# Causal attention: queries, keys and maxima brought to their rows by DMAs

## The chip, the cores and the metric

One core of a Trainium2 chip runs the whole program. The metric is the device time of one execution in microseconds (us), the median over runs of the same kernel. The engines are TensorE (PE in the profile; PEld is its weight load), VectorE (DVE), ScalarE (ACT), GpSimd (POOL) and SyncE (SP, which here only issues DMAs).

## The reference, cut to what matters

The program is a model of four layers; each adds two branches to x. Only the last layer's causal attention is touched:

```
q, k, v = heads(xn @ Wq.T), heads(xn @ Wk.T), heads(xn @ Wv.T)   # B = 2, S = 2048, 16 heads of 16
scores  = where(causal, q k^T * 16**-0.5, -inf)
out     = softmax(scores) v                                      # then the output projection, added to x
```

Beside it the layer's other branch ("phase") adds sqrt((xn cos)^2 + (xn sin)^2) to x.

## The kernel before, in words

Layer 3 (`layer3`, from line 2219) works through NJ = 8 groups j of four heads (four groups to each of the two sequences), and in each through NQ = 4 blocks n of 512 query positions. A pair (j, n) is called a unit here. Each unit is worked on twice.

`prep(j, n)` makes the unit's queries and keys and finds the row maxima of the scores. One product on PE (`pe_qk`, four PE instructions on f32 data) gives a 128x512 tile with 64 query rows and 64 key rows. ACT rounds it to fp32r (`hi`) and DVE takes the rest (`lo`), so that a product of 16-row heads can be made exactly enough from hi and lo parts. These rows then have to stand at other partitions: head hh of pair pr at partitions 64*hh onward of QS (queries) and KS (keys), as 16 rows each of hi, lo, hi for the queries and hi, hi, lo for the keys. `pe_place` does that with products by a selection matrix `Sel`: for each of queries (col 0) and keys (col 1), two pairs pr, and for each a product with hi and one with lo, so four products of 128x512 in a group; `act_place` evicts the two results of a group to QS or KS (and adds a one to the keys' spare rows). Then 8n+8 steps follow: in each, PE makes two 128 x up to 512 tiles of scores (two heads side by side, 64 rows of the array each) and DVE reduces each to its row maximum (L2592, and L2595 on the diagonal, with the causal mask `past`). Every maximum stands in a column of `pm`. At the end of a pair, `dve_maxima` writes the negated maxima into a wide bf16 tile `mz`, `pe_max` (L2358) turns them with four products by the identity, and `dve_max` (L2575) adds the resulting 128x512 tile from PSUM to the query rows, where row 48 of a head meets the ones of the keys. So the second pass gets score minus maximum from the product itself.

`main(j, n)` is the second pass: for each block kt of 128 keys up to the diagonal, four products K^T Q (64 rows of the array each, two side by side), four Exps on ACT (L2743), a causal mask on POOL for diagonal blocks, four products with the values (L2414), and at the unit's end the division by the sum and the output projection, added to x on DVE.

The order is written out by hand as generators. `weave_units` first runs `first()` (values, and prep of j = 0, all four n) beside the phase branch; then for each unit it weaves main(j, n) with prep(j+1, n) in fixed proportions; the last j has no prep beside it. `beside(n, step)` says what goes with which step of prep: at step 1 the next unit's qk product, at step 2 the maxima of the unit before (pair 1), at the half and one later the placing of the next unit's queries and keys, at half + 3 the maxima of pair 0. For n = 0 the unit's own placing stands in front of the steps, and for n = 3 no next unit is placed. All engines run their programs in order, and all products share a ring of seven PSUM banks (`psx`), each of which must be emptied before it is filled again. SP does nothing in this stage but store the output.

## Time and profile before

| | |
|---|---|
| median of 3 runs | 4099.81 us (4099.64 to 4100.76) |
| profiled execution | 4113.66 us, its span 4111.9 us |
| PE busy, of the span | 3689.5 us (90%) |
| DVE busy | 2578.5 us (63%) |
| ACT busy | 1742.1 us (42%) |
| POOL busy | 1087.5 us (26%) |
| granted PE clock, mean | 0.943 |
| attention, from the first placing to the end | 2962.8 us to 4111.9 us |

Busy time is the time in which an engine had an instruction under way. A window row gives the same for one stretch, with the count of instructions behind it and the granted clock of PE (1.00 is 2.4 GHz, and a mean below 1 is a mixture with 1.2 GHz). All times in the rows below are from the span's start.

### The profile page before, as it was taken

To read this page: it belongs to the slowest core of one execution; us is meant where nothing else is said; L and a number is where in the kernel's file an instruction comes from. 1 tells how busy PE (TensorE), PEld (TensorE's weight loads), DVE (VectorE), ACT (ScalarE), POOL (GpSimd) and SP (SyncE) were. 2 spreads that over 40 slices of the span, in tenths; PEclk is the share of its full clock that TensorE was granted. 3 is DMA by queue.
4 is the path that set the end of the run, shared out by engine and by line. 5 is a ranking of instruction groups with operands and counts; after the bars stand their busy time and mean duration, and the time that the engine had idled before them with its cause. 6 is when DMAs were issued, how large, how long until landed. Compare 5 with 4: busy or idle time off the path is not lost.

```text
span 4111.9 us, 47352 instructions
## 1 busy us (share of the span) xinstructions
PE 3689.5 (90%) x16820; PEld 2091.3 (51%) x16820; DVE 2578.5 (63%) x6523; ACT 1742.1 (42%) x3213; POOL 1087.5 (26%) x1140
## 2 busy tenths in 40 slices
PE   8899999787999898898859999999899999999997
PEld 7477777445544444454435555565543443444332
DVE  3534343646888977787754344442587888778881
ACT  2344333232343334333423333332226766666767
POOL 0611111602555545454512222222111010011001
PEclk7999999888999999899979999999899999999999
DMA  4356554204555646555510000000000000000000
GB/s 153 136 173 207 202 203 159 78 29 138 185 186 188 209 155 185 183 188 181 185 69 3 0 0 1 1 0 0 21 1 1 1 1 1 16 6 1 1 1 21
DMA packets 96157, 356.61 MB, mean 87 GB/s; under 512 B 15440, under 2 KB 42720, under 8 KB 85936
## 3 DMA queue, kind: packets, MB, share of 16 engines
q0 software_dynamic: 57328, 301.90, 22.6%
q1 hardware_dynamic: 37504, 49.58, 3.6%
q8 instruction: 133, 2.18, 0.2%
q10 hardware_dynamic: 1088, 2.10, 0.1%
q14 instruction: 104, 0.85, 0.1%
HBM read 322.32 MB, written 31.20 MB: 86 GB/s over the span
## 4 chain that ended last, share of the span: by engine, by line
PE 62%; DVE 24%; ACT 7%; issue 3%; POOL 3%; DMA 1%; POOLq 0%; SPq 0%; ACTq 0%; DVEq 0%
PE ps L171 48%; PE ps L2414 5%; DVE pm L2592 4%; PE ps L1947 2%; DVE gathB L1606 2%; PE ps L1429 2%; DVE hacc L1590 2%; ACT P L2743 2%; DVE mi L1548 2%; DVE ps L2595 1%; POOL xs_sorted L1147 1%; DVE tm L1506 1%; DVE fa L1856 1%; PE ps L2000 1%; DVE mx L1544 1%
## 5 line engine op out<-in xcount | busy, mean ns | idle before, releaser
L2743 ACT ACTIVATE P<-ps 128x512 f32<-128x512 f32 (+3 forms) x1280 | 589.2, 548 | 202.2 <-PE ps L171 199.5
L2592 DVE TENSOR_REDUCE pm<-ps 128x1 f32<-128x512 f32 x768 | 484.1, 685 | 82.1 <-PE ps L171 78.8
L1745 POOL DMA_INDIRECT gathB<-in_tab,idx x256 | 280.9, 1097 | 455.7 <-PE ps L1429 386.5
L2791 POOL TENSOR_SCALAR_AFFINE_SELECT P<-P 128x256 f32<-128x256 f32 x256 | 103.3, 407 | 911.0 <-ACT P L2743 907.1
L1745 POOL DMA_INDIRECT gathA<-in_tab,idx x256 | 272.8, 1066 | 226.9 <-DVE gte L1562 149.3
L171 PE MATMUL ps<-KS,QS 64*128 64x512 f32 (+3 forms) x1280 | 304.2, 424 | 21.4 <-DVE QS L2575 4.9
L2414 PE MATMUL ps<-P,Va 128*32 128x512 f32 (+3 forms) x2560 | 300.0, 541 | 11.3 <-POOL P L2791 6.3
L171 PE MATMUL ps<-QS,KS 64*128 64x512 f32 (+3 forms) x1280 | 283.4, 412 | 10.2 <-DVE xT L2543 4.6
L171 PEld LDWEIGHTS ps<-KS,QS 64*128 64x128 f32 x1280 | 139.7, 184 | 252.7 <-DVE pm L2592 69.5
L171 PE MATMUL ps<-f,K 128*128 128x512 f32 x1024 | 253.4, 399 | 13.9 <-POOL f L2205 11.3
L2595 DVE CUSTOM_DVE_ANT_0 ps<-ps,past 128x128 f32<-128x128 f32 (+3 forms) x512 | 240.7, 514 | 38.7 <-PE ps L171 37.6
L171 PE MATMUL ps<-WS,xn 128*128 128x512 f32 x512 | 236.8, 603 | 0.0
L171 PEld LDWEIGHTS ps<-QS,KS 64*128 64x128 f32 x1280 | 141.4, 185 | 187.2 <-issue 58.0
L171 PEld LDWEIGHTS ps<-f,K 128*128 128x128 f32 x1024 | 191.6, 188 | 69.6 <-POOL f L2205 17.1
L171 PE MATMUL ps<-xsT,FW 128*128 128x128 f32 x1704 | 205.1, 278 | 5.3 <-DMA FW<-in_F,fidx 5.3
L171 PEld LDWEIGHTS ps<-xsT,FW 128*128 128x128 f32 x1704 | 199.0, 194 | 5.7 <-issue 5.7
L1138 POOL DMA_INDIRECT FW<-in_F,fidx x71 | 71.5, 1007 | 445.7 <-PE ps L171 221.6
L2089 DVE CAST f<-fa 128x512 fp32r<-128x512 f32 x64 | 39.5, 638 | 223.0 <-ACT fa L2172 223.0
L1590 DVE SCALAR_TENSOR_TENSOR hacc<-gathA,lin,hacc 128x512 f32<-128x512 f32 x224 | 168.3, 751 | 7.0
L1544 DVE TENSOR_REDUCE mx<-ps 128x4 f32<-128x512 f32 x128 | 87.6, 684 | 127.7 <-PE ps L171 127.6
L2205 POOL TENSOR_TENSOR f<-fa,f 128x512 fp32r<-128x512 f32 x64 | 87.5, 1381 | 297.3 <-DVE f L2089 297.3
L1606 DVE CUSTOM_DVE_ANT_0 gathB<-hg,gathB 128x512 f32<-128x512 f32 x256 | 163.1, 690 | 2.8 <-DMA gathB<-in_tab,idx 2.8
(366 smaller groups left out, 7172.5 us busy)
## 6 DMA issues: line engine op xcount, KB each, us to landing
xs_sorted<-zero SPq DMA_DIRECT2D x1, 9088.0 KB, 33.0
xs<-xs_sorted SPq DMA_DIRECT2D x71, 128.0 KB, 2.2
ys_sorted<-ys SPq DMA_DIRECT2D x71, 128.0 KB, 1.7
gathA<-in_tab,idx POOLq DMA_INDIRECT x256, 5.5
gathB<-in_tab,idx POOLq DMA_INDIRECT x256, 5.1
out<-xT SPq DMA_DIRECT2D x8, 512.0 KB, 3.1
xT<-in_x SPq DMA_DIRECT2D x4, 512.0 KB, 9.6
xT<-in_x ACTq DMA_DIRECT2D x4, 512.0 KB, 8.6
```

The source lines that it names most:

```text
L171: m = pe.matmul(out, w, x, start=start and i == 0, stop=stop and i == len(pairs) - 1, skip_group_check=True)
L1429: pe.matmul(p[:, ms], GB[:, h, 512 + m * 128:640 + m * 128], dg[h], start=False, stop=h == 7, skip_group_check=True).then_inc(*PR.pe.tick( ...
L1544: dve.tensor_reduce(mx[:, 4 * g:4 * g + 4, 0], p[:, :].rearrange("p (i k) -> p i k", i=4), AX.X, ALU.max).then_inc(*PR.dve.tick("mx", t, g))
L1590: dve.scalar_tensor_tensor(out=hacc[:, :], in0=GA[:, h, 256:768], scalar=lin[:, h:h + 1], in1=src, op0=ALU.mult, op1=ALU.add).then_inc(*(P ...
L1606: dve.tensor_tensor_reduce(out=GB[:, h, 0:512], in0=hg[:, :], in1=GB[:, h, 0:512], scale=1.0, scalar=0.0, op0=ALU.mult, op1=ALU.add, accum ...
L1745: pool.indirect_dma_start(out=(GA, GB)[half][:, h, :], out_offset=None, in_=d[f"tab{half}"], in_offset=bass.IndirectOffsetOnAxis(ap=idx[t ...
L2205: pool.tensor_tensor(f1[:, 1, m, :], fa[:, m % 3, :], f1[:, 0, m, :].bitcast(F32), ALU.subtract).then_inc(*BN.pool.tick("f1", n, m))
L2414: m = pe.matmul(o_[32 * hd:32 * hd + 32, off:BW], Va[:, kt, h * 17:h * 17 + 32], Pb[2 * (kt % 2) + hd // 2][:, hd % 2, off:BW], start=kt = ...
L2592: v = dve.tensor_reduce(m, p, AX.X, ALU.max)
L2595: v = dve.tensor_tensor_reduce(out=p, in0=p, in1=past[:, 512 - w:512], scale=1.0, scalar=-3.0e38, op0=ALU.add, op1=ALU.max, accum_out=m)
L2743: act.activation(P_[:, hh, off:BW], psx.tile("s2", j, n, kt, pr, hh)[:, off:BW], ACT.Exp).then_inc(*psx.emptied(MN.act, "s2", j, n, kt, pr ...
L2791: pool.affine_select(out=P_, in_=P_, compare_op=ALU.is_ge, fill=0.0, base=0, pattern=[[0, 2], [1, 128]], channel_multiplier=-1).then_inc(* ...
```

## The change

The four-row-block placing is done by 24 DMAs a unit, issued by SP, straight from hi and lo to QS and KS. The selection matrix, its products and their evictions are gone. The factor 0.25 goes into the query weights. Zeros and ones that the placing used to write into spare rows are set once, by POOL, at the layer's start; for that QS and KS are moved to where nothing of the layer's first part lies. hi and lo have three buffers in place of two, and qk is made two units ahead instead of one. The maxima of a unit (16 rows of 128 after one product) are copied by DVE to `ms` and brought into one row of QS for each head by four DMAs. The score products read 48 rows of the array's 64 (first pass) and 49 (second pass).

```diff
-            QS/KS first, hi, lo x2, mz = [128, 16, 128] bf16 x2, Sel, kone
+            mz = [sb(f"mz{i}", [128, 2, 2, 4], BF16) for i in range(2)]
+            ms = [sb(f"ms{i}", [16, 128], F32R) for i in range(2)]
+            hi, lo = ([... F32R) for i in range(3)] ...)       # QS, KS now last
+                def place(j, n):
+                    bs = slice(n * BW, (n + 1) * BW)
+                    sp.wait_ge(*WT.pool.has("KS1"))
+                    sp.wait_ge(*MN.pe.has("s2", j - 2, 3, 4 * n + 3, 1, 1))
+                    sp.wait_ge(*PP.dve.has("qk", j, n))
+                    for col, to, places in ((1, KS, ((hi, 0), (hi, 16), (lo, 32))), (0, QS, ((hi, 0), (lo, 16), (hi, 32)))):
+                        for pr in range(2):
+                            for hh in range(2):
+                                r = 64 * col + 32 * pr + 16 * hh
+                                for from_, o_ in places:
+                                    o_ += 64 * hh
+                                    sp.dma_start(to[j % 2][o_:o_ + 16, pr, bs].bitcast(F32), from_[at(j, n)][r:r + 16, :].bitcast(F32)).then_inc(
+                                        *PL[at(j, n)].tick(j, n, col, pr, o_))
+                def shift(j, n):
+                    sp.wait_ge(*PP.dve.has("max", j, n))
+                    for pr in range(2):
+                        for hh in range(2):
+                            row = QS[j % 2][64 * hh + 48:64 * hh + 49, pr, n * BW:(n + 1) * BW].bitcast(F32)
+                            sp.dma_start(row.rearrange("o (q p) -> o q p", q=4),
+                                         ms[n % 2][8 * pr + 4 * hh:8 * pr + 4 * hh + 4, :].bitcast(F32)).then_inc(
+                                *MX[n % 2].tick(j, n, pr, hh))
+                for u in range(NJ * NQ + 2):
+                    if u < NJ * NQ:
+                        place(*divmod(u, 4))
+                        if u // 4 == 5:
+                            result(u % 4)
+                    if u > 1:
+                        shift(*divmod(u - 2, 4))
...
-                return {1: "qk", 2: "max1", half: "place0", half + 1: "place1", half + 3: "max0"}.get(step)
+                return {1: "qk", 2: "max"}.get(step)            # qk now of unit u + 2
...
-            def pe_place(pe, j, n, col): ...                    # and act_place, both gone
+            def pe_max(pe, j, n):
+                p = psx.fill("max", j, n)
+                pe.wait_ge(*PP.dve.has("mxs", j, 1, n))
+                pe.wait_all(psx.freed("max", j, n))
+                pe.matmul(p[0:16, 0:128], mz[n % 2][:, :, :, :].rearrange("p a b c -> p (a b c)"), identb[:, :], ...)
...
-                            pe.wait_ge(*PP.act.has("place", j, 0, n, 1))
-                            pe.wait_ge(*PP.act.has("place", j, 1, c, 1))
+                            pe.wait_ge(*placed(j, n))            # all 24 DMAs of the unit have landed
-                                rs = slice(64 * hh, 64 * hh + 64)
+                                rs = slice(64 * hh, 64 * hh + 48)
...
-                        pe.wait_ge(*PP.dve.has("max", j, 1, n))
+                        pe.wait_ge(*shifted(j, n))               # in main; rows 64*hh to +49 there
...
             def dve_start(dve):
-                kone, Sel: one 128x1024 and twelve 128x32 operations
+                dve.wait_ge(*W3A.total())
+                dve.tensor_scalar(WQK[:, :, :, 0:64], WQK[:, :, :, 0:64], 0.25, None, ALU.mult).then_inc(*WT.dve.tick("quarter"))
...
             def dve_qk / act_qk:
-                wait for place of the unit two before
+                wait_ge(*placed_before(j, n))                    # the DMAs of the unit three before
...
             def dve_max(dve, j, n):
-                dve.tensor_tensor(qs, qs.bitcast(F32), psx.tile("max", j, pr, n), ALU.add)     # twice a unit
+                dve.wait_ge(*shifted(*divmod(4 * j + n - 2, 4)))
+                dve.wait_ge(*PP.pe.has("max", j, n))
+                dve.tensor_copy(ms[n % 2][:, :], psx.tile("max", j, n)[0:16, 0:128])           # once a unit
...
+                pool.memset(QS[i][:, :, :].bitcast(F32), 0.0)    # i = 0, 1, before the layer's norm has ended
+                pool.memset(KS[i][:, :, :].bitcast(F32), 1.0).then_inc(*WT.pool.tick(f"KS{i}"))
```

`first()` makes qk of units 0 and 1 before the values. With the placing gone the weave's proportion is (12n+13)/(8n+10).

## Rows read from the trace of the kernel before

**Rows 1.** Windows: first prep stretch, woven stretch, last group; busy us and instructions, clock, DMA.

```profile
2963.00:3091.00 128.00, 118.11 (x349) 51.32 (x347) 104.22 (x258) 39.03 (x65) 19.08 (x15) 0.93 0.00 1
3091.00:4012.00 921.00, 877.04 (x5265) 369.98 (x5266) 741.19 (x1805) 628.38 (x1341) 90.39 (x224) 1.00 0.01 3
4012.00:4105.00 93.00, 78.52 (x510) 23.45 (x507) 9.03 (x14) 78.03 (x174) 12.86 (x32) 0.97 0.05 18
```

**Rows 2.** Windows of four woven units, n = 0 to 3, in the same columns.

```profile
3219.80:3237.20 17.40, 16.50 (x98) 8.14 (x98) 11.38 (x40) 12.12 (x28) 3.25 (x8) 1.00 0.00 1
3237.20:3264.10 26.90, 25.61 (x158) 10.77 (x158) 21.33 (x58) 18.61 (x41) 3.25 (x8) 1.00 0.01 2
3264.10:3302.90 38.80, 37.09 (x220) 14.82 (x219) 31.68 (x74) 26.54 (x57) 3.21 (x8) 1.00 0.00 1
3302.90:3349.00 46.10, 43.95 (x276) 17.50 (x274) 40.99 (x88) 32.56 (x69) 3.20 (x8) 1.00 0.00 1
```

**Rows 3.** Chain of waits by line: the unit n = 1, then the unit n = 3.

```profile
by line: PE ps L171 47.0%; PE ps L2414 18.5%; DVE pm L2592 15.8%; DVE ps L2595 7.9%; DVE QS L2575 4.3%; DVE lo L2561 2.6%; ACT hi L2692 2.3%; PE ps L2358 1.5%; issue 1.3%; DVE pm L2595 1.1%
by line: PE ps L171 40.6%; PE ps L2414 25.9%; DVE pm L2592 21.2%; DVE ps L2595 3.6%; ACT P L2743 2.4%; PE ps L2358 1.6%; DVE lo L2561 1.5%; issue 1.4%; ACT hi L2692 1.3%; ACT osb L2753 1.3%; DVE pm L2595 0.5%; ACTq L116 0.0%
```

**Rows 4.** Timeline, PE: a group of placing and a group of maxima (start, duration, what).

```profile
3414.63 0.50 PE L171 MATMUL ps<-hi,Sel 128*128 128x512 f32 x1
...
3415.76 0.50 PE L171 MATMUL ps<-QS,KS 64*128 64x512 f32 x2
...
3421.72 0.40 PE L2358 MATMUL ps<-identb,mz 128*128 128x128 bf16 x4
3422.05 0.64 PE L2414 MATMUL ps<-P,Va 128*32 128x512 f32 x4
```

**Rows 5.** Timeline, PE: the own placing of a unit n = 0, two groups together.

```profile
3219.99 0.50 PE L171 MATMUL ps<-hi,Sel 128*128 128x512 f32 x1
...
3221.96 1.08 PE L171 MATMUL ps<-osb,selS 128*128 128x512 f32 x2
```

**Rows 6.** Groups of instructions from 2963 us on: busy us, mean ns, idle before.

```profile
L2575 DVE TENSOR_TENSOR QS<-QS,ps 128x512 fp32r<-128x512 f32 x64 | 43.6, 681 | 4.5 <-PE ps L2358 4.5
L2700 ACT ACTIVATE KS<-ps,kone 128x512 fp32r<-128x512 f32 x64 | 41.0, 698 | 2.6 <-PE ps L171 2.6
L2702 ACT ACTIVATE QS<-ps 128x512 fp32r<-128x512 f32 x64 | 35.1, 606 | 8.4 <-PE ps L171 8.4
```

**Rows 7.** Timeline, DVE, at the layer's start: a copy, and Sel's twelve operations.

```profile
2882.42 0.22 DVE L2483 COPY selS<-ident 128x128 f32<-128x128 f32 x1
...
2883.27 1.12 DVE L2492 TENSOR_SCALAR Sel<-ident 128x32 fp32r<-128x32 f32 x12
```

**Rows 8.** Timeline, all engines: PE's first work in the layer, and POOL's idle time before.

```profile
2888.26 4.27 PE L171 MATMUL ps<-xT,onesm 128*128 128x512 f32 x5 [8.64 <-DMA aWo<-in_aWo]
2940.72 3.94 POOL L2800 MEMSET Va<- 128x4608 f32 x1 [58.40 <-DVE xn L295]
```

**Rows 9.** Timeline: placing of the first unit, and the first lo.

```profile
2943.41 0.69 DVE L2561 TENSOR_TENSOR lo<-ps,hi 128x512 fp32r<-128x512 f32 x1 [2.41 <-ACT hi L2692]
...
2962.78 0.79 PE L171 MATMUL ps<-hi,Sel 128*128 128x512 f32 x1
...
2966.21 0.33 PE L171 MATMUL ps<-KS,QS 64*128 64x128 f32 x2 [1.00 <-ACT KS L2700]
```

**Rows 10.** Window of ten us in the first prep stretch, columns as in Rows 1.

```profile
3053.00:3063.00 10.00, 9.69 (x22) 3.75 (x22) 7.87 (x18) 1.83 (x3) 1.26 (x1) 0.84 0.00 0
```

**Rows 11.** Timeline, SP's queue: DMA issues in the layer's start, four of 16 rows first.

```profile
2882.51 1.71 SPq L2261 DMA_DIRECT2D aWo<-in_aWo  x4
2884.27 0.42 SPq L2263 DMA_DIRECT2D th<-in_theta  x1
```

**Rows 12.** Timeline, SP's queue at the program's start, DMA engines full.

```profile
9.15 1.17 SPq L458 DMA_DIRECT2D Wo<-in_Wo  x1
```

**Rows 13.** DMA issues: KB each, median us from issue to landing.

```profile
aWo<-in_aWo SPq DMA_DIRECT2D x4, 64.0 KB, 3.9
```

More of the change, by code:

```diff
@@ L2224, in layer3 @@
             WQK = sb("aWqk", [128, 2, 4, 128])
-            Sel = sb("Sel", [128, 8, 128], F32R)
             Wvn = sb("aWv", [128, 2, 256])
-            kone = sb("kone", [128, 1])
             past = sb("past", [128, 512])
@@ L2248, in layer3 @@
             NQ, NJ = 4, 8
+            PL = [load(f"place{i}") for i in range(3)]
+            MX = [load(f"maxima{i}") for i in range(2)]
             W3A, W3O, W3T = load("w3a"), load("w3o"), load("w3t")
@@ L2263, in sp, with result @@
                     sp.dma_start(th4[i][:, :, :], d[n_]).then_inc(*W3T.tick(n_))
-                for n in range(NB):
+                def result(n):
                     sp.wait_ge(*XT.has("attn", 4 * (n // 4) + 3, n % 4, 1))
                     sp.dma_start(both(out, n), both(xT, n)).then_inc(*OUT.tick(n))
+                def place(j, n):
[26 more added lines that the diff above has]
+                        shift(*divmod(u - 2, 4))
+                for n in range(4, NB):
+                    result(n)
                 sp.wait_ge(*OUT.total())
@@ L2279, in weave_units @@
                         if j + 1 < NJ:
-                            weave((main(j, n), 1.0), (prep(j + 1, n), (12 * n + 13) / (8 * n + 13 + 2 * (n == 0))))
+                            weave((main(j, n), 1.0), (prep(j + 1, n), (12 * n + 13) / (8 * n + 10)))
                         else:
@@ L2288, in beside, with at, placed, shifted @@
             def beside(n, step):
-                half = 4 * n + 4
-                return {1: "qk", 2: "max1", half: "place0", half + 1: "place1", half + 3: "max0"}.get(step)
-            def following(j, n):
-                return (j, n + 1) if n + 1 < NQ else (j + 1, 0)
+                return {1: "qk", 2: "max"}.get(step)
+            def at(j, n):
+                return (4 * j + n) % 3
+            def placed(j, n):
+                return PL[at(j, n)].has(j, n, 0, 1, 96)
+            def shifted(j, n):
+                return MX[n % 2].has(j, n, 1, 1)
+            def placed_before(j, n):
+                return placed(*divmod(4 * j + n - 3, 4))
             def preceding(j, n):
                 return (j, n - 1) if n else (j - 1, NQ - 1)
+            def ahead(j, n):
+                return divmod(4 * j + n + 2, 4)
             class Tail:
@@ L2689, in act_qk @@
             def act_qk(act, j, n):
[L2690 removed]
+                act.wait_ge(*placed_before(j, n))
                 act.wait_ge(*PP.pe.has("qk", j, n))
[L2692 to L2703 removed]
+                act.activation(hi[at(j, n)][:, :], psx.tile("qk", j, n), ACT.Copy).then_inc(*PP.act.tick("hi", j, n))
             def act_prep(act, j, n):
[L2706 to L2709 removed]
                 for step in range(1, 8 * n + 9):
@@ L2712, in act_prep @@
                     also = beside(n, step)
-                    if also == "qk" and following(j, n)[0] < NJ:
-                        act_qk(act, *following(j, n))
-                    if also == "place0" and n + 1 < NQ:
-                        act_place(act, j, n + 1, 0)
-                    if also == "place1" and n + 1 < NQ:
-                        act_place(act, j, n + 1, 1)
+                    if also == "qk" and ahead(j, n)[0] < NJ:
+                        act_qk(act, *ahead(j, n))
                     if also:
```

115 lines of the change are left out of this document (27 added, 88 removed).

## The prediction, made before the result was known

> **What bounds the kernel now.** I read the windows first. The attention runs in three stretches: prep of the first group beside the phase branch (128 us), the woven stretch (921 us) and the last group alone (93 us) [rows 1]. In the woven stretch PE has an instruction under way for 877 of 921 us at full clock, DVE for 741, ACT for 628: PE is the nearest to its limit. One round of four units takes 17.4 + 26.9 + 38.8 + 46.1 = 129.2 us, and the seven rounds repeat almost to the tenth, so I work on one round [rows 2]. PE's idle share is 5% in each unit, but DVE's busy share climbs from 65% (11.38 of 17.4) over 79% and 82% to 89% (40.99 of 46.1) [rows 2]. The chain of waits says the same: for n = 1, lines of PE hold 67% and DVE's reductions (L2592, L2595) 25%; for n = 3 PE still holds 68%, but DVE's runs sit between PE's because the ring of banks is emptied by them [rows 3]. So: what leaves PE counts nearly in full for n = 0 to 2, and for n = 3 what leaves DVE counts. In the first stretch DVE is busy 104 of 128 us and PE's clock is 0.93 [rows 1]; in its late part PE runs at 0.84 [rows 10]. In the last stretch DVE has nothing to do and ACT is busy 78 of 93 us [rows 1]; no edit touches that, apart from fewer rows in the products.
>
> **Removed from PE.** A placing group of four products takes the slot from 3414.63 to 3415.76, 1.13 us [rows 4]. Each unit n = 0, 1, 2 places the next one, two groups, 2.26 us; n = 3 places nothing; n = 0 places itself first, in 3221.96 - 3219.99 = 1.97 us [rows 5]. A group of maxima takes 3422.05 - 3421.72 = 0.33 us [rows 4], two a unit; after the change one product of 16 columns of weights is left, for which I take 0.10 us (a quarter of the group is 0.08), so 0.56 us go. Per round: 1.97 + 3 x 2.26 + 4 x 0.56 = 11.0 us.
>
> **Removed from DVE and ACT.** DVE loses two additions of 0.68 us a unit [rows 6] and gains a copy of 16x128 from PSUM; the nearest row is the copy of 128x128, 0.22 us [rows 7]. Net 1.14 us a unit. ACT loses four evictions a unit, 2 x 0.70 + 2 x 0.61 = 2.6 us [rows 6], all of it beside PE's work; it makes room, no more.
>
> **What of that counts, per unit.** n = 0: PE frees 1.97 + 2.26 + 0.56 = 4.8 us of 17.4; DVE would then be at 10.2 of 12.6, so I take 4.2. n = 1 and 2: PE frees 2.82 each; DVE stays below 85%, I take 2.5 and 2.4. n = 3: PE frees 0.56, DVE 1.14; DVE's runs are on the path in part, I take 0.9. Per round 10.0 us, seven rounds 70 us. Bounds of this term: only what DVE loses, 4 x 1.14 x 7 = 32 us, and all of PE's, 77 us, with some 5 more if bank waits shrink.
>
> **The first stretch.** The first unit's placing holds PE from 2962.78 to 2966.21, of which the last 1.0 us is a wait for ACT [rows 9]: 3.4 us go, if the DMAs have landed by then (below). The next unit's placing, 2.26 + 0.56, falls in PE's share, 2.6 us. From n = 1 on DVE leads, and I count its 1.14 and a little of PE's per unit, 4 in all. Sum 10 us; bounds 5 (DVE alone) and 14 (all of PE's: 3.4 + 3 x 2.26 + 4 x 0.56 is 12.4, and a gain in clock). The qk product of unit 1 goes ahead of the values; it is moved, not added.
>
> **The layer's start.** DVE sheds Sel, which ends at 2884.4 [rows 7], long before PE's first product at 2888.26, which waits for the aWo DMA [rows 8]. Its new wait is for the aWqk and aWv DMAs, issued ahead of aWo on the same queue, so covered by that same wait; the scaling behind it is one operation of 128x512. POOL's four fills of 4096 columns cost 4 x 3.94 x 4096/4608 = 14 us, in a stretch in which it idled for 58 us [rows 8]. Both count 0; without cover they would cost 1 and 14 us. No DVE slowdown beside POOL is priced; up to 2 us at most if half of DVE's norm work in those 14 us ran a few tenths slower.
>
> **Added on SP: 28 DMAs a unit, 896 in all.** This is the one new resource, and the trace has no SBUF to SBUF copy. The nearest in shape are the four aWo loads, 16 rows of 4 KB: four issues in 1.71 us, the next starting 1.76 us after the first, so 0.44 us each [rows 11], landing 3.9 us after issue [rows 13]. So 24 placings take 10.6 us to issue and the unit's 28 take 12.3 us, against units of 13.2 to 45 us. Where they queue: a unit's placing is issued once its qk (two units ahead) and the previous shift are out. The tightest are the two placings that must wait for main to have read the old keys. In a round of the forecast (13.2, 24.4, 36.4, 45.2 us, 119.2 in all), n = 3 begins at 74.0; placing of the next round's unit 0 waits for key block 3 of 16, at 74.0 + 11.3 = 85.3; then come 24 DMAs, the 4 of the shift, and 24 more for unit 1, which is wanted at 119.2 + 13.2 = 132.4. With d us per DMA it is late by 85.3 + 52d + 3.9 - 132.4 = 52d - 43.2 us. At 0.44 that is 20 us early. In the first stretch placing starts after lo at 2944.1 and lands at 2944.1 + 10.6 + 3.9 = 2958.6, PE wants it at 2962.8 [rows 9]. So DMAs count 0. The new waits of ACT and DVE (placing three units before) are older than what prep itself has waited for. Behind PE's wait for a placing stands everything, main too, since PE is in order. d is unknown between 0.44 and the 1.17 us that an issue took with the DMA engines full [rows 12]; I take 0.44, since engines here are at 0.01 of their share [rows 1].
> The Trainium skill, "DMA: Bandwidth & Descriptors", section "Anatomy of one DMA", gives a fixed cost of about 2 us for each DMA, and under "Rules for kernel authors" says that under 64 KB one pays mostly overhead; these are 32 KB. Read as time that adds up in a row, 28 x 2 = 56 us a unit, an estimate by that page, it would put this kernel far behind; the page puts most of it down to completion, which overlaps, and the aWo issues at 0.44 us bear that out as far as the issue goes.
>
> **Fewer rows.** No row shows a product over 48 or 49 rows; the bounds are no change and the 64-row slot doubled by a lost pairing, which I hold for excluded since the two heads still start at rows 0 and 64. The Trainium skill, "TensorE: Matmul & The Clock Gate", section "LDWEIGHTS", says a weight load costs by columns and not by rows; by it this is 0.
>
> **Sum.** 70 + 10 = 80 us from the profiled 4113.66, giving 4033.7; the median of the runs lies 13.9 us below the profiled execution, so 4099.8 - 80 = 4020 us.
>
> **Rivals.**
> (A) DVE is the bound already and PE's gain comes back as waits for banks: only DVE's loss counts, 32 + 5 = 37 us, 4063; with half of the rest, 58 us, 4042. For it: 89% in n = 3 and DVE's places in the chain [rows 2, 3]. Against: n = 0 to 2 have 18% to 35% of DVE free.
> (B) All of PE's share counts, and waits for banks and for evictions with it: 82 + 14, 4004. For it: PE 95% busy in every unit. Against: n = 3.
> (C) SBUF to SBUF copies of 16 rows are slow, and PE waits for unit 1's placing in each round. Nothing is late below d = 0.83 us; the gain is gone at 52d - 43.2 = 80/7, d = 1.05; at 1.17 each round waits 17.6 us, 123 in all, and the first placing lands at 2944.1 + 28.1 + 3.9 = 2976, 13 us late: 4020 + 123 + 13 = 4156. For it: no row of such a copy, 32 KB between few partitions. Against: the 0.44 of the aWo loads.
> (D) PE's clock. It is 0.84 where PE waits for DVE in the first stretch [rows 10] and 1.00 in the woven one. With less work PE waits more; if the four rounds' n = 3 units went to 0.84, their 43 us of PE work would take 8 us more each, 57 in all: 4077. Against: n = 3 loses only 0.56 of its 44 us of PE work. The Trainium skill, "TensorE: Matmul & The Clock Gate", section "Part 1: The HAM clock gate", says the clock falls to half when the array idles; the 0.84 agrees, the 1.00 at 95% busy too.
> (E) The change does nothing for the time because DMAs hold up half the units and give the gain back: d about 1.05, inside (C)'s price.
>
> **How the numbers follow.** Forecast (4005 to 4035) 0.48; (B) 0.14; (A) 0.22; (D) 0.04; (C) 0.09; (E) 0.03. Differences under 0.2%, 8 us, are about what a measurement of this kernel can't tell from none. Faster by more: 0.48 + 0.14 + 0.22 + 0.04 = 0.88; same 0.03; slower 0.09. The range runs from (B)'s far side, 3994, to (A)'s end, 4064; it leaves out about 0.17, (C), (E), (D) and little below.
>
> **What would show it.** No products from Sel, and no 128x512 additions to QS; PE's busy time in the woven stretch down by some 75 us; units of about 13, 24, 36 and 45 us; SP issues at 0.44 us. PE waiting for DMA ahead of a score product, above all at the start of n = 1 units, would show (C) and make the forecast wrong; waits for pm (L2592) growing by tens of us would show (A).

## The result, and the profile after

The changed kernel takes 4057.41 us (median of 4 runs, 4049.19 to 4069.39), the kernel before beside it 4100.28 us (4099.64 to 4101.49): ratio 0.9897, 95% interval 0.9871 to 0.9924. That is 43 us off, where 80 were forecast. It is faster and inside the range, but about half of the gain is missing, and most of what follows is about that half. The forecast's own band was 4005 to 4035; 4057 lies outside it, in the part of the range that stood there for rival A.

The profiled execution took 4054.18 us (span 4052.4, mean clock 0.941), 59.5 us less than the profiled one of before. Split at the first `hi`, the first product of main and the end of the last woven unit:

| stretch | before | forecast | after | after - before |
|---|---|---|---|---|
| up to the first `hi` | 2942.8 | 2942.8 | 2932.3 | -10.5 |
| first stretch (prep of j = 0 beside the phase branch) | 148.5 | 138.5 | 151.1 | +2.6 |
| woven stretch | 918.1 | 848.1 | 866.3 | -51.8 |
| last group alone | 102.5 | 102.5 | 102.7 | +0.2 |

The 10.5 us ahead of the attention are not the change's: 9.9 of them are there when the layer before ends, in code that both kernels share. DVE's last operation of that layer, in the kernel before and after:

```profile
2879.66 1.54 DVE L2108 SCALAR_TENSOR_TENSOR xT<-ps,vec,xT 128x512 f32<-128x512 f32 x2 [2.62 <-PE ps L2000]
2869.74 1.54 DVE L2108 SCALAR_TENSOR_TENSOR xT<-ps,vec,xT 128x512 f32<-128x512 f32 x2 [2.63 <-PE ps L2000]
```

So this is scatter between executions (the profiled one of before lay 13.4 us above its median, the one of after 3.2 below). Inside the attention 49.0 us went, against 80: 12.6 us are missing in the first stretch, 18.2 in the woven one.

First the windows of the kernel after: the three stretches (the first one from PE's first score product on, as in [rows 1] from the first placing on), then the four units of the second round, in the columns of [rows 1].

```profile
2954.50:3083.40 128.90, 116.36 (x294) 48.60 (x293) 100.53 (x254) 29.66 (x49) 18.98 (x15) 0.89 0.13 29
3083.40:3949.70 866.30, 822.08 (x4838) 331.99 (x4838) 708.64 (x1769) 569.02 (x1229) 91.39 (x224) 0.98 0.12 27
3949.70:4052.40 102.70, 80.88 (x511) 24.42 (x511) 12.84 (x23) 78.63 (x175) 12.86 (x32) 0.96 0.06 21
3205.00:3218.90 13.90, 12.65 (x77) 5.25 (x77) 10.80 (x40) 7.94 (x21) 3.31 (x8) 1.00 0.08 17
3218.90:3244.00 25.10, 23.39 (x141) 9.43 (x140) 20.16 (x57) 16.14 (x37) 3.25 (x8) 1.00 0.21 47
3244.00:3279.00 35.00, 33.73 (x205) 13.53 (x204) 29.91 (x71) 24.59 (x53) 3.25 (x8) 1.00 0.04 9
3279.00:3325.60 46.60, 44.47 (x269) 17.55 (x268) 40.25 (x88) 32.89 (x69) 3.25 (x8) 1.00 0.16 34
```

What matters here are the units: 13.9, 25.1, 35.0 and 46.6 us, where [rows 2] have 17.4, 26.9, 38.8 and 46.1 and the forecast 13.2, 24.4, 36.4 and 45.2. n = 2 gained more than forecast, n = 3 got half a microsecond longer. PE's share of each is 91% to 96%, about as before; its busy time in the woven stretch fell by 55 us, where the prediction looked for some 75. And the clock of the woven stretch is 0.98, not the 1.00 of [rows 1]. Where that is, a second set of windows shows: the n = 1 unit of the third round, five of its slices, and the one long n = 2 unit.

```profile
3339.40:3366.10 26.70, 24.98 (x141) 9.64 (x142) 20.20 (x57) 16.15 (x36) 3.25 (x8) 0.94 0.22 48
3347.40:3348.40 1.00, 0.80 (x2) 0.44 (x3) 1.00 (x5) 1.00 (x3) 0.00 (x0) 0.95 0.21 49
3348.40:3349.40 1.00, 1.00 (x2) 0.00 (x0) 0.13 (x2) 0.38 (x1) 0.00 (x0) 0.50 0.27 57
3349.40:3350.40 1.00, 1.00 (x5) 0.20 (x8) 0.69 (x1) 0.00 (x0) 0.00 (x0) 0.50 0.18 41
3350.40:3351.40 1.00, 1.00 (x8) 0.00 (x0) 0.00 (x0) 0.00 (x0) 0.00 (x0) 0.50 0.29 64
3351.40:3352.40 1.00, 1.00 (x9) 0.61 (x6) 0.09 (x1) 0.25 (x1) 0.00 (x0) 0.84 0.02 4
3487.80:3525.80 38.00, 36.95 (x205) 14.18 (x206) 29.44 (x71) 24.80 (x53) 3.25 (x8) 0.90 0.03 7
```

The same 141 PE instructions take 26.7 us here and 25.1 in the round before. From about 3348.3 to 3351.7 the granted clock is 0.50, the 1.2 GHz level; around it it is 1.00. PE's timeline at that place, and then at the same place of the round before:

```profile
3346.88 0.87 PE L171 MATMUL ps<-KS,QS 48*128 48x256 f32 x2
3347.94 1.70 PE L171 MATMUL ps<-On,aWo 128*128 128x512 f32 x2 [0.20 <-ACT P L2738]
3349.57 1.94 PE L2443 MATMUL ps<-P,Va 128*32 128x512 f32 x8
...
3226.26 0.87 PE L171 MATMUL ps<-KS,QS 48*128 48x256 f32 x2
3227.32 1.10 PE L171 MATMUL ps<-On,aWo 128*128 128x512 f32 x2 [0.20 <-ACT P L2738]
3228.35 1.06 PE L2443 MATMUL ps<-P,Va 128*32 128x512 f32 x8
```

Same instructions, same wait of 0.20 us in front, but 1.70 and 1.94 us for what takes 1.10 and 1.06. In the 15 us before the fall PE had been busy without a gap of more than these 0.20 us, with two-head score products of 48 and 49 rows among others. Of the seven units n = 1 five are longer in this way (four by 1.6 us, one by 1.1), and of the units n = 2 one, by 3.0. The n = 1 unit that is 1.1 us longer and the n = 2 unit belong to one fall, the longest, from 3484.8 to 3495.0 us, and that one has longer waits of PE in front of it:

```profile
3479.65 0.32 PE L171 MATMUL ps<-KS,QS 48*128 48x128 f32 x1 [0.49 <-DVE pm L2607]
...
3482.18 0.38 PE L171 MATMUL ps<-KS,QS 48*128 48x256 f32 x1 [0.42 <-DVE pm L2607]
...
3484.55 0.32 PE L171 MATMUL ps<-QS,KS 49*128 49x128 f32 x1 [0.44 <-DVE pm L2607]
```

DMAs now. SP's timeline in a woven unit:

```profile
3291.62 1.19 SPq L2281 DMA_DIRECT2D KS<-hi  x2
3292.85 0.58 SPq L2281 DMA_DIRECT2D KS<-lo  x1
3293.48 1.22 SPq L2281 DMA_DIRECT2D KS<-hi  x2
```

The DMA issues, with KB each and median us to the landing:

```profile
KS<-hi SPq DMA_DIRECT2D x243, 32.0 KB, 2.0
```

PE's timeline at its only wait for one of them:

```profile
2965.62 0.49 PE L171 MATMUL ps<-KS,QS 48*128 48x512 f32 x2 [2.29 <-DMA QS<-hi]
```

One issue takes 0.59 us and the next starts 0.63 us after this one's start (three in 1.86 us, from 3291.62 to 3293.48); the copy has landed 2.0 us after its issue. In the woven stretch no PE instruction waits for a DMA. The tightest copy of this round, the last for the next unit n = 1, is issued here:

```profile
3324.52 0.59 SPq L2281 DMA_DIRECT2D QS<-hi  x1
```

With 2.0 us it has landed at 3326.5, and PE's first product that needs it starts at 3339.6, 13 us later. In the first stretch the second unit's scores wait 2.3 us: its 24 copies are issued behind the first unit's, 48 x 0.63 us from 2933.67 on.

The new small work, where [rows 4, 6] had 0.33 us and 0.68 us, each twice a unit, and a score product of 49 rows, in PE's timeline and then in DVE's:

```profile
3343.59 0.50 PE L171 MATMUL ps<-QS,KS 49*128 49x512 f32 x2
...
3345.24 0.22 PE L2399 MATMUL ps<-identb,mz 128*16 128x128 bf16 x1
```

```profile
3346.12 0.27 DVE L2593 CAST ms<-ps 16x128 fp32r<-16x128 f32 x1
```

I had taken 0.10 us for the product, which holds PE for 0.17 (from 3345.24 to the next product at 3345.41), and 0.22 us for the copy. Both are off by little.

### The profile page after: what moved, and what is told of

Same layout as the page of the kernel before. It is cut to its first block, busy times and chain, and to the rows that moved or that the text cites. A ratio compares the mean times of both kernels' runs of the same rounds, so it can differ in the third digit from the quotient of the medians.

```text
span 4052.4 us, 47260 instructions
## 1 busy us (share of the span) xinstructions
PE 3629.4 (90%) x16340; PEld 2040.0 (50%) x16340; DVE 2544.9 (63%) x6478; ACT 1674.9 (41%) x3085; POOL 1100.8 (27%) x1142
## 3 DMA queue, kind: packets, MB, share of 16 engines
q8 instruction: 130, 2.13, 0.2%
## 4 chain that ended last, share of the span: by engine, by line
PE 61%; DVE 24%; ACT 6%; issue 4%; POOL 3%; DMA 1%; SPq 1%; POOLq 0%; ACTq 0%; DVEq 0%
PE ps L171 47%; PE ps L2443 5%; DVE pm L2607 5%; PE ps L1947 2%; DVE hacc L1590 2%; DVE gathB L1606 2%; PE ps L1429 2%; DVE mi L1548 2%; ACT P L2738 2%; POOL xs_sorted L1147 1%; DVE ps L2610 1%; DVE tm L1506 1%; DVE fa L1856 1%; PE ps L2000 1%; DVE mx L1544 1%
## 5 line engine op out<-in xcount | busy, mean ns | idle before, releaser
L171 PE MATMUL ps<-KS,QS 48*128 48x512 f32 (+3 forms) x1280 | 336.4, 420 | 29.5 <-DVE pm L2607 16.9
L171 PE MATMUL ps<-QS,KS 49*128 49x512 f32 (+3 forms) x1280 | 289.0, 414 | 14.0 <-DVE pm L2607 9.8
L171 PEld LDWEIGHTS ps<-KS,QS 48*128 48x128 f32 x1280 | 158.8, 186 | 245.7 <-DVE pm L2607 96.7
L171 PE MATMUL ps<-f,K 128*128 128x512 f32 x1024 | 254.7, 401 | 13.9 <-POOL f L2205 11.4
L171 PEld LDWEIGHTS ps<-QS,KS 49*128 49x128 f32 x1280 | 140.3, 187 | 218.7 <-ACT P L2738 72.3
L2610 DVE CUSTOM_DVE_ANT_0 ps<-ps,past 128x128 f32<-128x128 f32 (+3 forms) x512 | 239.4, 512 | 14.6 <-PE ps L171 13.2
```

The costliest lines, as they stand in the source:

```text
L171: m = pe.matmul(out, w, x, start=start and i == 0, stop=stop and i == len(pairs) - 1, skip_group_check=True)
L2610: v = dve.tensor_tensor_reduce(out=p, in0=p, in1=past[:, 512 - w:512], scale=1.0, scalar=-3.0e38, op0=ALU.add, op1=ALU.max, accum_out=m)
```

## The experiments

The measure beside the ratio is the length of the stretches as in the table above (first, woven) and of the units of an undisturbed round (in e7 n = 3 is at a clock of 0.97 in nearly all rounds, and in e10 n = 1 and 2 hold waits for DMAs). Chips differ by up to 2.4% in the time before, so ratios are compared, each with before on its own chip.

| | ratio (95%) | first | woven | round n = 0, 1, 2, 3 |
|---|---|---|---|---|
| before | 1 | 148.5 | 918.1 | 17.5 26.8 38.8 46.1 |
| after | 0.9897 (0.9871 to 0.9924) | 151.1 | 866.3 | 13.9 25.1 35.0 46.6 |
| e1 placing only | 0.9924 (0.9909 to 0.9939) | 157.8 | 875.2 | 14.9 25.5 35.7 46.7 |
| e2 maxima only | 0.9967 (0.9954 to 0.9980) | 151.9 | 905.6 | 17.1 26.7 38.1 45.6 |
| e3 phase weave 1.5 | 0.9856 (0.9837 to 0.9874) | 147.1 | 863.2 | 13.9 25.1 35.0 46.6 |
| e4 old proportion | 0.9933 (0.9919 to 0.9948) | 151.1 | 884.6 | 14.5 25.3 36.4 47.1 |
| e5 after, second chip | 0.9880 (0.9864 to 0.9896) | 151.1 | 866.4 | 13.9 25.1 35.0 46.6 |
| e6 64 rows | 0.9856 (0.9836 to 0.9876) | 151.8 | 855.6 | 13.9 25.1 35.0 46.6 |
| e7 maxima later | 0.9887 (0.9870 to 0.9903) | 153.2 | 873.9 | 13.9 24.8 35.2 49.0 |
| e8 empty steps in n = 3 | 0.9894 (0.9878 to 0.9910) | 151.2 | 868.7 | 13.8 25.1 35.0 45.8 |
| e9 64 rows in main only | 0.9863 (0.9832 to 0.9895) | 153.8 | 860.1 | 13.9 25.1 35.0 46.6 |
| e10 placing DMAs halved | 1.0348 (1.0328 to 1.0368) | 188.0 | 1024.3 | 13.9 45.4 43.6 46.6 |
| e11 e3 + e8 + e9 | 0.9830 (0.9805 to 0.9854) | 142.6 | 856.4 | 13.8 25.1 35.0 45.8 |
| e12 e3 + e8 + e6 | 0.9804 (0.9786 to 0.9822) | 140.8 | 851.4 | 13.8 25.1 35.0 45.8 |

**e1 and e2: which half of the change gives what.** e1 has the placing by DMAs and keeps the maxima of before (four products, two additions a unit); e2 has the reverse. Each has the weave's proportion fitted to the steps that it has left (8n+11 and 8n+12 in the divisor, 2 more in e2 for n = 0), so neither is the removed work alone.

```diff
 e1:                pe.wait_ge(*placed(j, n))
+                   pe_max(pe, *preceding(j, n), 1), pe_max(pe, j, n, 0)      # as before
 e2:                pe_place, act_place, Sel as before
+                   return {1: "qk", 2: "max", half: "place0", half + 1: "place1"}.get(step)
```

> Queries and keys placed by DMA as in the change, the maxima as before (eight products and two 128x512 additions a unit; row 48 of the queries then also keeps the maxima of the earlier groups of the same buffer, a constant a row that cancels in the softmax). If PE's share is what counts, the placing alone (8.75 us of PE a round) gives the larger part: 30 to 45 us under the kernel before. If DVE is the bound (rival A), it gives next to nothing, 0 to 10 us, since no DVE work leaves.

> Placing by products on PE as before, the maxima by one product, one copy and four DMAs a unit. By the PE account 2.24 us a round leave PE and 4.6 us DVE: 10 to 20 us under the kernel before. If DVE is the bound, this alone gives nearly all of what the whole change gives, 35 to 45 us.

Measured: e1 4080.79 us and e2 4096.81 us beside 4109.03, so 28 and 12 us off (31 and 13.5 at the chip of the first result by the ratios), together 45 where after has 43. In the woven stretch e1 takes 43 us off and e2 12.5, together 55, and after 52: there the parts add up. In the first stretch they don't: e1 is 9.3 us longer there than before and e2 3.4, after 2.6. e1's clock is 0.87 there, against 0.94 before and 0.91 in after; why e1 is the worst was not tried. Rival A, in which only DVE's loss counts, is out: e1 leaves DVE all of its additions, and n = 0 to 2 still give 2.6, 1.3 and 3.1 us. For n = 3 it is otherwise, as the windows of e1 show, units n = 1 and n = 3:

```profile
3237.40:3262.90 25.50, 23.37 (x148) 9.15 (x147) 21.14 (x56) 16.20 (x37) 3.21 (x8) 1.00 0.21 48
3298.60:3345.30 46.70, 44.56 (x276) 17.58 (x275) 41.09 (x89) 32.90 (x69) 3.26 (x8) 1.00 0.15 35
```

And of e2, unit n = 0:

```profile
3207.10:3224.20 17.10, 16.64 (x91) 7.71 (x93) 10.13 (x36) 12.07 (x29) 3.26 (x8) 1.00 0.01 2
```

e1's n = 3 has the 276 PE instructions of [rows 2] and takes 46.7 instead of 46.1 us. Taking nothing out of PE there, and placing elsewhere, costs 0.6, while e2 gains 0.5 there: the order in the ring of banks or the weave's proportion, which e4 and e8 look at. One thing no run takes apart: each placing group that went had not only PE's time but also two banks of the ring and two evictions on ACT, and what n = 0 to 2 gained may be partly theirs.

**e3 and e4: the two weaves.** The proportion of main and prep was changed with the kernel, that of the first stretch wasn't, though `first()` lost steps.

```diff
 e3:
-                weave((first(), 1.0), (phase(), 1.75))
+                weave((first(), 1.0), (phase(), 1.5))
 e4:
-                (12 * n + 13) / (8 * n + 10)
+                (12 * n + 13) / (8 * n + 13 + 2 * (n == 0))
```

> The changed kernel with the phase branch woven at 1.5 in place of 1.75 steps for one of the first group's prep. Theory W: prep of the first group has 96 steps now (110 before) beside 64 steps of phase, so at 1.75 the phase branch (112) is left over alone at the end; at 1.5 both end together and 6 to 12 us come back. Theory K (PE's clock at 0.83 in this stretch is the whole loss): 0 to 3 us.

> The changed kernel with the proportion of main and prep as it was, (12n+13)/(8n+13), and 2 more for n = 0, so that prep's steps come denser and end before main does. If the order of products in the bank ring is what keeps the n = 3 units at 46.6 us, this moves them: 10 us either way. If DVE's or PE's work alone sets them, the same or 1 to 5 us slower, since main's last blocks then run alone.

Measured: e3 takes 4 us from the first stretch (151.1 to 147.1), between what the two theories gave (6 to 12 and 0 to 3). One profile each is thin for 4 us, since e9, whose first stretch has the same instructions as after's, came out 2.7 us longer. The woven stretch, in which e3 changes nothing, is 3.1 us shorter: it has fewer falls of the clock, and at other places. e3's ratio is better than after's, 0.9856; the profiles give 7 us of that and the ratios 17, so part of the gap is scatter. e4 makes every unit longer and the woven stretch 18.3 us, much more than the 1 to 5 us that I had expected if work alone set the units. So the new proportion is not where n = 3 lost its time; it is worth 18 us of the 52.

**e5 and e6: the rows of the score products, and the clock.** e5 is the kernel after once more, on the second chip; in e6 the products read 64 rows as before.

```diff
-                                rs = slice(64 * hh, 64 * hh + 48)      # prep; main has + 49
+                                rs = slice(64 * hh, 64 * hh + 64)      # both
```

> The changed kernel itself, on the chip of the runs beside it: 0.985 to 0.993 of the kernel before, with single runs up to 20 us apart, and units n = 1 of either 25.1 us (clock 1.00) or 26.7 us (clock 0.94) in a mixture that differs from run to run.

> The changed kernel with its score products over 64 rows of the array again instead of 48 and 49 (the spare rows hold zeros against ones, and in the first pass old maxima, which cancel in the softmax). Theory R: fewer rows let PE's clock fall; then the first stretch goes back to 0.93 and no n = 1 unit runs at 0.94, 10 to 20 us less. Theory G (the clock falls because PE now waits more, whatever the rows): no difference within 3 us.

Measured: e5 has the same units as after to the tenth, the long ones too, so the falls of the clock aren't chance, and my expectation of a mixture that differs from run to run was wrong. In e6 no woven unit n = 1 or n = 2 is longer than 25.2 and 35.1 us, the woven stretch is 10.8 us shorter than e5's and its clock 1.00. The medians on this chip are 4131.59 and 4122.41 us, 9.2 us apart, though their single runs overlap. Windows of e6, the first stretch, the woven stretch, and the units n = 1, 2 and 3 of a round:

```profile
3010.40:3162.20 151.80, 139.47 (x375) 64.34 (x374) 108.57 (x273) 33.24 (x55) 22.14 (x17) 0.89 0.14 32
3162.20:4017.80 855.60, 810.57 (x4838) 329.79 (x4838) 708.46 (x1769) 568.81 (x1228) 91.81 (x224) 1.00 0.12 28
3296.10:3321.10 25.00, 23.28 (x141) 9.33 (x140) 20.09 (x57) 16.11 (x36) 3.27 (x8) 1.00 0.21 46
3321.10:3356.20 35.10, 33.81 (x205) 13.62 (x206) 30.02 (x72) 24.65 (x53) 3.27 (x8) 1.00 0.04 10
3356.20:3402.80 46.60, 44.44 (x269) 17.56 (x268) 40.27 (x88) 32.93 (x69) 3.27 (x8) 1.00 0.16 34
```

Where the clock holds, a unit is as long with 48 rows as with 64: the rows cost nothing in the product itself, only by the clock. PE's busy time in the woven stretch is 810.57 against 822.08 of after, which is all of the difference. The added rows hold nothing that counts (zeros against ones, and in the first pass row 48 with a constant of each query), so it is the reading of the rows that matters here. (The kernel before could not read fewer: by its code the third block of 16 rows stands at row 48 and the maxima in row 32, not in row 48 as told above.) In the first stretch more rows do nothing (151.8 us at 0.89), against theory R.

The other runs say how far this goes. In rounds two to seven no unit is below full clock in before, e2, e6 and e12, which read 64 rows in both passes, nor in e11, which does in main alone; e9, with e11's rows, has two such units. With 48 and 49 rows there are five such units in after and in e5, two in e3, four in e4, six in e7 and seven in e8, but none in e1, which has the same rows and more products (e10 is left out, since PE waits for DMAs there). So in these runs the falls in these rounds come only with narrow rows, but narrow rows alone don't bring them, and e3, whose woven stretch is that of after, shows that their number and place also hang on when the stretch begins. Nor is a fall beside a busy PE new with the change: [rows 10] have the clock at 0.84 with PE busy for 9.69 of 10 us, at 64 rows.

**e7 and e8: n = 3.** e7 takes the maxima two steps later; e8 has three steps of prep without products in n = 3, where before had two empty steps (16, 17) and the maxima of pair 0 (19), with the proportion moved to fit, so that main's products fall in other places of the ring.

```diff
 e7:
-                return {1: "qk", 2: "max"}.get(step)
+                return {1: "qk", 4: "max"}.get(step)
 e8:
+                n == 3: {1: "qk", 2: "max", 16: "none", 17: "none", 19: "none"}
+                proportion (12 * n + 13) / (8 * n + 10 + 3 * (n == 3))
```

> The changed kernel with the product and the copy of the maxima at step 4 of the next unit's prep in place of step 2. At step 2 the product fills the very bank of the ring that qk used one step earlier, so PE waits for lo: 25 us in the waits of the changed kernel. If that wait is on the path, 10 to 20 us less; if PE then only waits at the next product, 0 to 3 us.

> The changed kernel with three empty places in the prep of n = 3 (steps 16, 17, 19), where the kernel before had them too, so that the order of products against main is nearly that of before in these units. If the order in the ring is what makes n = 3 46.6 us although 0.56 us of PE and 1.1 us of DVE work left it, they come to 45.0 to 45.6 us, 7 to 11 us less in all; if not, 46.6 stays.

Measured: e7 shortens n = 1 by 0.3 and lengthens n = 3 by 2.4 us, with no work added or taken, where I had expected a gain or nothing. Of the 2.4 us most is the clock, which is at 0.97 in that unit; the one n = 3 unit of e7 in rounds two to six that ran at full clock took 47.4 us, 0.8 more than in after:

```profile
3743.20:3790.60 47.40, 44.70 (x269) 17.57 (x268) 40.29 (x88) 32.87 (x68) 3.27 (x8) 1.00 0.15 33
```

e8 takes 0.8 us from n = 3 (46.6 to 45.8), a little less than the 1.0 to 1.6 expected, and gains nothing in all, because more units run at the low clock: n = 0 twice at 16.5, n = 1 at up to 27.5 us. The chain of waits by line of an n = 3 unit, of after, beside [rows 3]:

```profile
by line: PE ps L171 43.2%; PE ps L2443 27.3%; DVE pm L2607 23.4%; ACT P L2738 2.6%; DVE ps L2610 2.6%; issue 1.4%; DVE mz L2587 0.4%; DVE pm L2610 0.3%; PE ps L2399 0.1%; ACTq L116 0.0%
```

The same of e8:

```profile
by line: PE ps L171 34.9%; DVE pm L2607 27.8%; PE ps L2443 19.6%; ACT P L2738 11.0%; DVE ps L2610 3.7%; ACT hi L2706 1.3%; issue 1.3%; ACT inv L2724 1.1%; DVE pm L2610 0.5%; ACTq L116 0.0%
```

Both chains alternate between PE's products and DVE's reductions, as in [rows 3]. What e7 and e8 show is that in n = 3 the order alone moves the unit by -0.8 to +0.8 us at full clock, about as much as the 1.7 us of PE and DVE work that the change took out.

Where that time sits can be read from PE's timeline. PE's idle time in an n = 3 unit is the same before and after (2.15 and 2.13 us, from the windows). What grew is the time that the score products hold, counted from the start of each to the start of PE's next instruction: 25.9 us before, 26.9 after. The two products of a pair of heads mostly start together and run side by side; in 11 of the 64 pairs the second one starts more than 0.15 us late in before, in 16 of 64 in after, and in 11 of 64 again in e8, where the score products hold 26.1 us. e6 has after's 16 and 26.8, so this has nothing to do with the rows. The same count for the other units, before and after, is 5.1 and 6.1 us for n = 0, 12.2 and 13.3 for n = 1, 20.2 and 19.3 for n = 2. Which pair meets which bank of the ring was not followed.

**e9: whose rows.** As e6, with 64 rows in main's products alone.

```diff
-                            rs = slice(64 * hh, 64 * hh + 49)
+                            rs = slice(64 * hh, 64 * hh + 64)      # main only
```

> The products of main's scores over 64 rows again instead of 49, prep's stay at 48; nothing else differs from the kernel after. Run e6 had 64 rows in both and no unit with a dip of the clock (every n = 1 unit 25.1 us, every n = 2 unit 35.0, woven stretch 10.8 us shorter). Theory R1, the rows of main's products carry it, since main's score products are wide (up to 512 columns) and stand closest together: all n = 1 units 25.1 us, woven stretch about 856 us, ratio about 0.986 as in e6. Theory R2, it is the sum of rows over all products: prep's are about as many columns, so half of the dips are left: some n = 1 units at 26.7 us, woven about 861 us, ratio about 0.987. Theory R3, prep's rows carry it: as the kernel after, woven 866 us, ratio 0.988 to 0.990.

Measured: woven 860.1 us, every round as in e6 but one (125.8 us, with units of 26.2 and 38.0). Of 10.8 us 6.3 came back with main's rows alone, which is nearest to R2. The split is not a fine one: all that is left in e9 is one long fall, and e11, with the same rows, has none in these rounds.

**e10: rival C made to happen.** Each placing copy in two halves, same bytes.

```diff
-                                    sp.dma_start(to[...][o_:o_ + 16, pr, bs] ...)
+                                    for half in range(2):
+                                        sp.dma_start(to[...][o_:o_ + 16, pr, n * BW + 256 * half:n * BW + 256 * half + 256] ...)
```

> Each placing DMA cut into two of 256 columns (16 rows of 1 KB): the same bytes, twice the DMAs, 48 + 4 a unit. It tests what I held of rival C, that a unit in round is late by 52d - 43.2 us. If the issue is paid by the DMA (0.59 us each, starting every 0.63 us, as the kernel after shows), a former placing costs d = 1.26 us: with the rounds as measured (unit n = 3 begins at 74.0 of 120.6 us, key block 3 of 16 at 85.7, wanted at 134.5) unit n = 1 of each round waits 85.7 + 48 x 1.26 + 2.3 + 2.0 - 134.5 = 16 us, seven times 112 us; in the first stretch the second unit's placing lands at 2934.5 + 96 x 0.63 + 2 = 2997 instead of 2967, 30 us later. In all about 4057 + 112 + 30 = 4200 us on the first chip, ratio to before 1.02 (1.00 to 1.03, since the phase and other units take up part of it). If the issue is paid by the bytes (0.3 us for 16 KB), nothing changes: ratio 0.989.

Measured: 4327.12 us beside 4185.82, ratio 1.0348. SP's timeline, and behind it the DMA issues:

```profile
3314.96 2.45 SPq L2283 DMA_DIRECT2D KS<-hi  x4
3317.45 1.22 SPq L2283 DMA_DIRECT2D KS<-lo  x2
```

```profile
KS<-hi SPq DMA_DIRECT2D x512, 16.0 KB, 1.8
```

PE's waits for DMAs in the woven stretch (us in all, times, longest), and one of them in its timeline:

```profile
PE ps L171 <- DMA QS<-hi: 127.2, 13, 18.2
```

```profile
3346.44 0.80 PE L171 MATMUL ps<-KS,QS 48*128 48x512 f32 x2 [17.73 <-DMA QS<-hi]
```

The windows of its units n = 1 and n = 2:

```profile
3328.40:3373.80 45.40, 26.08 (x141) 10.21 (x139) 20.25 (x57) 16.26 (x36) 3.25 (x8) 0.77 0.10 25
3373.80:3417.40 43.60, 36.63 (x205) 14.22 (x206) 30.05 (x72) 24.74 (x52) 3.25 (x8) 0.88 0.09 23
```

An issue of 16 KB takes as long as one of 32 KB (four of them in 2.49 us to the next, 0.62 us each, against 0.63): it is paid by the DMA. The lateness formula of the prediction gave 16 us for each unit n = 1, and the trace shows 17.7 in the round above and 18.2 at most. What it left out is twofold: the unit n = 2 waits too (5.9 us), and behind a wait the clock is low (0.77 and 0.88), so that n = 1's PE work takes 26.08 instead of 23.39 us and n = 2's 36.63 instead of 33.73. In all 195 us more than after in the two stretches, where I expected 142, and the ratio is above the 1.00 to 1.03 that I had given. So rival C was a real threat, and twice the DMAs were enough to turn the gain into a loss of 3.5%.

**e11 and e12: the findings together.**

```diff
 e11: e3's 1.5, e8's empty steps, e9's 64 rows in main
 e12: e3's 1.5, e8's empty steps, e6's 64 rows in both
```

> Three findings together on the kernel after: phase weave 1.5 instead of 1.75 (e3: first stretch 4 us shorter), three empty steps in unit n = 3 of prep (e8: n = 3 0.8 us shorter, but more dips of the clock in other units), and 64 rows in main's products (e9: nearly all dips gone). Theory S, the gains add up since the rows take away what the empty steps brought back: first stretch 147 to 150 us, rounds of 13.9 + 25.1 + 35.0 + 45.8 = 119.8, woven 850 to 855 us, ratio to before 0.983 to 0.985. Rival, the dips of e8 come from the order of n = 3 and stay: n = 1 units at 26.7 us or more, woven 860 us or more, ratio 0.986 to 0.988.

> As e11, with 64 rows in prep's products too (row 48 of the queries there still holds the minus maximum of two heads before, a constant of each query that goes through to the next maximum; rows 49 to 63 are zeros). Theory S: as e11, without the one late round with dips that e9 had (125.8 instead of 120.6 us), so woven 848 to 852 us and ratio 0.982 to 0.984. Rival, prep's rows do nothing: equal to e11 within 0.1%.

Measured: e12 takes 4116.05 us beside 4197.29, ratio 0.9804 (0.9786 to 0.9822), the fastest of all and 0.8% to 0.9% under the kernel after (e5, first result), a little better than the 0.982 to 0.984 expected; e11 0.983 as expected. The intervals of the two overlap, so whether prep's rows add anything in this pair is unclear. Windows of e12: first stretch, woven stretch, units n = 1 and n = 3.

```profile
3015.00:3155.80 140.80, 131.77 (x375) 62.03 (x374) 104.70 (x265) 33.60 (x55) 22.13 (x17) 0.93 0.16 34
3155.80:4007.20 851.40, 806.85 (x4839) 326.93 (x4838) 711.70 (x1778) 565.55 (x1228) 91.07 (x224) 1.00 0.12 28
3290.60:3315.70 25.10, 23.36 (x141) 9.43 (x142) 20.18 (x57) 16.16 (x36) 3.25 (x8) 1.00 0.21 47
3350.80:3396.60 45.80, 43.66 (x269) 17.04 (x268) 40.20 (x88) 32.48 (x69) 3.20 (x8) 1.00 0.15 32
```

The empty steps' falls of the clock are gone with 64 rows, as theory S has it, apart from the first round (e11 16.5 and 28.4 us, e12 15.0 and 25.1). The first stretch came out shorter than expected, 140.8 us at a clock of 0.93, where the same stretch of before, from the first `hi` on, has 0.94. Of the 10 to 11 us 4 go to the phase weave by e3; the empty steps fall into `first()` too, and whether they give the rest or scatter does, no run tells.

## Why the prediction was right in sign and range, and half off in size

The sign and the main idea hold: work that leaves PE shortens the units. That the number fell inside the range is partly luck. The forecast's own band missed, and 4057 lies where rival A had put it, for reasons that are not rival A's.

1. **Unit by unit.** Forecast 4.2, 2.5, 2.4 and 0.9 us off, undisturbed 3.6, 1.7, 3.8 and -0.5: 8.6 a round, not 10.0. For n = 0 to 2 together 9.1 of the 10.4 us taken out of PE came back as time. What I had wrong was to hold the work that stays for fixed: the score products hold 1.0, 1.1 and 1.0 us more in n = 0, 1 and 3 and 0.9 less in n = 2 than before, and with that the units come out within 0.2 us of what PE lost (4.8 - 1.0, 2.8 - 1.1, 2.8 + 0.9 and 0.6 - 1.0). The proportion of the weave moved with the change, and e4 shows it is worth 2.8 us a round; with the old one n = 0 to 2 give 6.9 us. I had left this edit unpriced. The prediction also says that the seven rounds repeat almost to the tenth; rounds two to seven of before take 127.5 to 143.5 us, and only three of them 129.2 or 129.3.
2. **n = 3: the step that failed in the woven stretch.** I took 0.9 us for what leaves DVE and PE; the unit got 0.5 us longer. The term was read as work removed (e2, which takes the maxima's work alone, does give 0.5 us), while e1, e7 and e8 show that the order counts for as much there: five more pairs of score products are pulled apart. Seven times 1.4 us are 9.8 us; the rounds of j = 4 and j = 6 gave 0.7 and 1.7 us more than the others, so the undisturbed woven stretch (e6, 855.6) lies 7.5 us above the forecast's 848.1.
3. **"Fewer rows": the other step that failed.** I counted 0, and for the product itself that holds: the product of 49x512 takes 0.50 us a pair like that of 64x512 in [rows 4], the weight load of 48 rows 186 ns in the mean against 184 for 64. But the clock fell in units in which PE is busy for 93% and 96% of the time: 866.3 against 855.6 us. The Trainium skill, "TensorE: Matmul & The Clock Gate", section "LDWEIGHTS", is right on the load and says nothing against the fall; the section "Part 1: The HAM clock gate" puts the fall down to idling, and here most falls came behind a gap of 0.20 us that was there without a fall a round earlier, and they went when the operands had 64 rows again. My rival D looked for it in n = 3 units, by less work; it came in n = 1 and n = 2, with narrower work, and cost 10.7 us, not 57. D's reading of [rows 10] was wrong too: I took the 0.84 for a place where PE waits for DVE and said that it agrees with the section, but PE is busy for 9.69 of those 10 us.
4. **The first stretch.** Forecast -10, measured +2.6. The 3.4 us of the first placing went, but 2.3 came back as the wait for the second unit's copies: I had computed the landing of the first unit (15.8 us behind the first `hi`; it was about 18) and not that of the second, which queues behind it. 4 us are the phase weave left at 1.75 (e3). The clock is 0.89 where [rows 1] have 0.93. The whole stretch before and after, from the first `hi` on:

```profile
2942.80:3091.30 148.50, 138.34 (x430) 66.28 (x428) 111.77 (x276) 42.03 (x70) 25.69 (x19) 0.94 0.00 0
2932.30:3083.40 151.10, 138.56 (x377) 64.22 (x375) 108.57 (x273) 33.23 (x55) 22.07 (x17) 0.91 0.15 32
```

PE has 53 instructions fewer and is busy for as long. By these clocks it spent some 27 us at the 1.2 GHz level instead of 18, which is worth up to 5 us, an estimate from these two rows. What brings the clock down there no run shows; the rows don't (e6). e12 has 140.8 us, near the 138.5 forecast, so the work did leave; the pacing and the clock ate it.
5. **DMAs.** Cost 0 in the woven stretch: right, with another margin than I thought. d is 0.63 us, not 0.44; by my formula 52 x 0.63 - 43.2 = -10.4, so 10 us early instead of 20; read from the trace it is 13. The landing is 2.0 us, not 3.9. The Trainium skill gives a fixed cost of about 2 us ("DMA: Bandwidth & Descriptors", section "Anatomy of one DMA"), measured there on DMAs that GpSimd issues, which the prediction didn't say. The landing of 2.0 us behind SyncE's issue is close to it, and it does overlap: the next issue starts 0.63 us on.
6. **Rival A** (4042 to 4063) gives a number close to the measured 4057, but its mechanism, DVE's loss alone, is refuted by e1: the total lands there for other reasons. Rival B is out by n = 3. What e12 reaches, ratio 0.9804, is the forecast's own 4020 / 4099.8 = 0.9805, with three further edits that the change did not have.
7. **The layer's start** cost nothing that can be seen: from the start of that last operation of the layer before to the first `hi` it is 63.1 us before and 62.6 after.

In sum: of the 31 us missing in the attention, 10.7 are the clock with fewer rows (after against e6, with e5 as the repeat), 7.5 the sizes of the units, n = 3 above all (shown in size; which products meet is open), 4 the phase weave (one profile, and that much only if no scatter is in it), 2.3 the wait for the second unit's copies (read from the trace, not tried without), and the remaining 6 the low clock and pacing of the first stretch, whose cause is not settled. The medians differ by 43 and not 49 us; that rest is within the scatter of after's runs (4049 to 4069).

## What to carry to other kernels

When work is taken out of a woven order, reprice every proportion and place that counted on it, the ones in other stretches too; here the old proportion would have cost a third of the gain in the woven stretch (18 of 52 us). And look whether the work that stays still runs as before: here pairs of products that had run side by side came apart. Small SBUF to SBUF copies on an idle queue are free up to a point that can be computed: count the DMAs between the moment that buffers come free and the moment the data is wanted, times 0.63 us, add the 2.0 us of the landing, and do so for every unit, the second of the first stretch among them. Before narrowing a product's contraction, look whether it buys any time; where it buys none, leave zeros in, as e6 does.

## What the hardware did that I had not expected

- The granted clock fell to its 1.2 GHz level in the midst of a stretch in which PE had been busy with no gap above 0.20 us for 10 us (one fall, the longest, came behind waits of up to 0.49 us). It did so at the same places in the two profiles of the same kernel on two chips (after and e5), at fewer and other places when only the stretch ahead was changed (e3), and not at all once the score products read 64 rows instead of 48 and 49 (e6). It cost 10.7 us in seven rounds.
- An issue on SP's queue takes 0.59 us for an SBUF to SBUF copy of 16 rows, 32 KB or 16 KB alike, against 0.43 us for the loads of [rows 11], and the copy lands 2.0 (32 KB) and 1.8 us (16 KB) after it.
- A unit with a 17.7 us wait for a DMA took 20.3 us longer (45.4 against 25.1, e10); the clock over that unit was 0.77.
